# Attention stage of a graph kernel: three waits put among GpSimd's gathers of a group

## The chip, the cores and the metric

One core of a Trainium2 chip runs the whole program. The metric is device time in microseconds (us) from start to end of the program on that core; a lower number is better. Engines are named as in the profile: PE (TensorE), PEld (its weight loads), DVE (VectorE), ACT (ScalarE), POOL (GpSimd), SP (SyncE). "SPq" and "ACTq" are the DMA-issuing instructions of SP and ACT.

## The reference

A graph of 6250 nodes (128 numbers each) and 200000 edges sorted by destination goes through two layers. Only the second, attention over each node's incoming edges, is touched here:

```python
x_l = (x @ W).reshape(N, H, C)                       # H = 4 heads, C = 32
logits = leaky_relu(a_src[src_all] + a_dst[dst_all] + a_edge, 0.2)
m = segment_max(logits, dst_all)
p = exp(logits - m[dst_all])
alpha = p / segment_sum(p, dst_all)[dst_all]
out = segment_sum(alpha[:, :, None] * x_l[src_all], dst_all) + bias
```

So each edge needs the row `x_l[src]` of its source (with `a_src` beside it, 132 float32 numbers, 528 bytes), weighs it, and adds it to the sum of its destination.

## The kernel before

The edges are cut in chunks of 128 (one edge to a partition), and 15 chunks (`J`) make a group; there are 108 groups. The stage `attention` treats one group in each call of `step`; `steps` runs 8 rounds of 12 such calls in a hardware loop and the last 12 written out. Each engine has its own `step`, and they meet only in semaphores.

What one group needs, in the order of the data:

- **The source rows**, into `G`, which holds four groups. 14 or 15 chunks of a group are fetched by POOL: one indirect DMA for a chunk, 128 rows of 528 bytes, the line `pool.indirect_dma_start(...)` (L2317). One chunk of every third group is fetched by SP instead (`row_in`, L2246), as 128 DMAs of one row, with the offset of each read from a list into a register first; SP also loads the list of places of each group (`rows_of`, L2265). Two more groups of twelve have a chunk fetched in the same way by ACT, 22 rows in each step.
- **The logits** `L`: DVE adds the gathered `a_src` to what PE spread before (L2617). It waits there for all chunks of the group.
- **The running maxima** along edges of one destination: PE turns `L`, DVE scans it (L2624, L2627), PE fetches its ends (L2472, L2473), DVE reads them into `rows` (L2640) and links the chunks (L2644, L2646), PE turns back, ACT makes the exponentials.
- **The messages** `MSG`: DVE multiplies the gathered rows by the weights (L2513), as the first instruction of the next `step`.
- **The sums**: PE multiplies the messages of a chunk by its one-hot matrix (L2449), three chunks to a bank of PSUM, five banks to a group. `s_m` counts finished banks. In PE's step of group g the banks 0, 1 and 2 of group g - 1 are made in the middle and bank 3 at the very end; bank 4 follows in the next step. DVE adds each chunk to `ACC` (L2542); its first such addition for group g - 1 waits for that group's bank 0.

POOL's step for group g waits for two things: its indices (`s_i`, copied by ACT at L2392 in step g - 3) and the free place in `G` (`s_ms`, the messages of group g - 4). Then it issues all its gathers in a row. So POOL works three groups ahead of DVE. Its queue holds nothing else in this stage.

`hold` is a wait followed by an instruction that does nothing.

Of the kernel before, what the change touches and what calls it, by code (L numbers as in the profile page):

```python
# [41 lines left out]
J = 15  # L42
TRI = 3
NT = J // TRI
# [49 lines left out]
def hold(eng, semaphore, value):  # L94

    eng.wait_ge(semaphore, value)
    eng.nop(nofuse=True)
# [54 lines left out]
def build(nc, x, src, dst, edge_attr, W1l, W1r, b1, W2l, W2r, b2, gamma, beta,  # L152
          W, W_edge, att_src, att_dst, att_edge, bias, out):
    with ExitStack() as top:
# [9 lines left out]
        def sem(name, at, gathers=False):  # L164

            for n in itertools.count():
                h = at.enter_context(nc.semaphore(f"{name}_{len(stages)}" + n * "_"))
                assert h.num not in stale
                if kinds.setdefault(h.num, gathers) == gathers:
                    used.append(h.num)  # L170
                    return h
# [1932 lines left out]
        def attention(at, block):  # L2104
# [22 lines left out]
            s_m = sem("a_m", at)  # L2127
# [80 lines left out]
            END = MAX_CHUNKS - (N_GRP - 1) * J  # L2208
# [5 lines left out]
            def chunk_apart(u):  # L2214

                if u % BY_SP == BY_SP - 1:
                    return 0
                return J - 1 if u % UN in BY_ACT else None

            def places(u):  # L2220

                apart = chunk_apart(u)
                at_ = (0, J + 1, 2 * J + 3, 3 * J + 4)[u % 4] + (1 if apart is None else 0 if apart == 0 else 2)
                return G[:, at_:at_ + J, :]

            def gathered(u, last=J):

                return [j for j in range(last) if j != chunk_apart(u)]
# [9 lines left out]
            def offsets(kind, to):  # L2238

                _, v = nc.values_load_multi_w_load_instructions(  # L2240
                    to, engines=(kind,), min_val=0, max_val=(NV - 1) * ROW,
                    skip_runtime_bounds_check_because="the sources are numbers of nodes, times a row's bytes")
                return v
# [5 lines left out]
            def steps(eng, body):  # L2249

                rounds = N_GRP // UN - 1
                with eng.Fori(0, rounds) as i:
                    for u in range(UN):
                        body(i, u, UN * i + u, None)
                for u in range(UN):
                    body(rounds, u, UN * rounds + u, UN - 1 - u)
# [53 lines left out]
            @block.gpsimd  # L2310
            def _(pool):

                def step(i, u, g, left):
                    pool.wait_ge(s_i, g + 1)
                    hold(pool, s_ms, g + 1)
                    for j in gathered(u, END if left == 0 else J):
                        pool.indirect_dma_start(  # L2317
                            places(u)[:, j, :], None, x_tab, bass.IndirectOffsetOnAxis(
                                ap=idx[:, u % 4, j:j + 1], axis=0)).then_inc(s_g[u % 4], 16)
                pool.memset(BLK[:], 0).then_inc(s_bz, 1)  # L2320
                hold(pool, s_i, 2)
                pool.indirect_dma_start(places(1)[:, chunk_apart(1), :], None, x_tab, bass.IndirectOffsetOnAxis(
                    ap=idx[:, 1, chunk_apart(1):chunk_apart(1) + 1], axis=0)).then_inc(s_g[1], 16)
                steps(pool, step)
# [180 lines left out]
            def _(dve):  # L2505
# [18 lines left out]
                def blocks(g, at_, to=None):  # L2524

                    _, v = nc.values_load_multi_w_load_instructions(
                        BLK[0:1, bass.ds(g + 2, 1), at_:at_ + 8], engines=DVE_ONLY, min_val=0, max_val=NB - 1,
                        skip_runtime_bounds_check_because="a block's number counts blocks begun so far, less one")
                    if to is None:
                        blk[at_:at_ + 8] = v  # L2530
                    else:
                        to[at_:at_ + 8] = v
# [296 lines left out]
```

## Time and profile before

| | |
|---|---|
| median of 3 runs | 4956.41 us (4937.31 to 4965.21) |
| the profiled execution | 4993.1 us |
| its span, first to last instruction | 4991.3 us |
| granted TensorE clock, mean | 0.690 |
| busy: PE, DVE, ACT, POOL | 49%, 52%, 32%, 38% |
| attention stage, first to last group's messages (L2513) | 1610.3 to 4926.5 us of the span |

Two thirds of the span is the attention stage; before it lie the first layer and the projections, after it a short last stage. In the page's 40 slices DVE is at 40% and PE at 20 to 30% throughout the attention stage, POOL at 40%. A busy share of 40% says that neither engine is full; which wait ends last in a group has to be read from the timeline of one group.

### The profile page before, as it was taken

The page shows a single profiled execution, that of the slowest core. Times are in us where ns is not written, and L with a number is a line of the kernel's source. Part 1 is how long each engine was busy: PE and PEld are TensorE (multiplying, and loading weights), DVE is VectorE, ACT ScalarE, POOL GpSimd, SP SyncE. Part 2 cuts the span into 40 slices and gives each one's busy share as a digit, 9 for nine tenths or more (in the row PEclk, how much of TensorE's full clock was granted, in tenths as well). Part 3 has the DMA queues.
Part 4 walks back from the last instruction along what each step waited for, and adds up shares of the span by engine and source line. Part 5 has one row for each costly group of instructions (what it writes and reads, how often), then busy time and mean ns, then how long its engine had stood idle before and what let it go on. Part 6 is the DMA issues. An engine that isn't in the chain of part 4 may idle for free. (4 is left out here: it accounts for less than half of the span.)

```text
span 4991.3 us, 76533 instructions
## 1 busy us (share of the span) xinstructions
PE 2467.1 (49%) x19840; PEld 2062.6 (41%) x19840; DVE 2605.1 (52%) x7011; ACT 1609.9 (32%) x2523; POOL 1873.3 (38%) x1919
## 2 busy tenths in 40 slices
PE   3699999998994323323323333333333333333333
PEld 3587777877773223223223222222232322322223
DVE  2599999476754444434434444444444444444446
ACT  2487778545552212112112111111211121211121
POOL 3501113113324444444444444444444444444441
PEclk9899999999996555555555555555555555555555
DMA  3233347168883111111111111111111111111113
GB/s 114 70 160 137 150 153 177 68 226 249 252 253 123 48 52 48 47 48 52 46 48 52 46 49 49 50 47 51 50 45 52 49 46 51 49 46 52 50 47 73
DMA packets 181876, 433.71 MB, mean 87 GB/s; under 512 B 48877, under 2 KB 106074, under 8 KB 173054
## 3 DMA queue, kind: packets, MB, share of 16 engines
q1 hardware_dynamic: 68832, 273.22, 15.0%
q0 software_dynamic: 64944, 126.25, 12.2%
q10 hardware_dynamic: 47630, 28.97, 2.1%
q8 instruction: 174, 2.85, 0.2%
q14 instruction: 296, 2.42, 0.2%
HBM read 308.89 MB, written 120.97 MB: 86 GB/s over the span
## 5 line engine op out<-in xcount | busy, mean ns | idle before, releaser
L2317 POOL DMA_INDIRECT G<-x_tab,idx x1557 | 1477.3, 949 | 1859.7 <-ACT idx L2392 1393.0
L2449 PE MATMUL pu<-MSG,OH 128*128 128x140 f32 x3282 | 788.9, 415 | 118.5 <-issue 65.4
L2542 DVE TENSOR_TENSOR ACC<-pu,ACC 128x140 f32 x1641 | 486.2, 296 | 592.2 <-remote 380.6
L2449 PEld LDWEIGHTS pu<-MSG,OH 128*128 128x128 f32 x3282 | 714.6, 306 | 132.9 <-issue 73.4
L2345 ACT CAST ADG<-pt 128x180 bf16<-128x180 f32 x108 | 102.4, 948 | 1856.6 <-remote 1057.9
L2466 PE MATMUL pc<-ident,L 128*60 128x128 f32 x108 | 42.3, 391 | 867.9 <-issue 482.5
L973 ACT CAST AE<-psA 128x784 bf16<-128x784 f32 x496 | 396.6, 815 | 174.6 <-PE psA L1006 135.4
L2640 DVE COPY rows<-pc 1x120 f32<-1x120 f32 x108 | 29.2, 270 | 789.7 <-remote 717.2
L2483 PE MATMUL pc<-ident,cin 1*60 1x1 f32 x216 | 37.1, 239 | 807.6 <-DVE cbk L2646 664.8
L1107 DVE TENSOR_TENSOR OHL<-iol,LH 128x2048 bf16<-128x2048 bf16 (+1 forms) x248 | 358.1, 1444 | 71.8 <-remote 33.6
L2466 PEld LDWEIGHTS pc<-ident,L 128*60 128x60 f32 x108 | 13.7, 127 | 900.8 <-issue 900.8
L2483 PEld LDWEIGHTS pc<-ident,cin 1*60 1x60 f32 x216 | 28.0, 185 | 832.6 <-DVE cbk L2646 684.8
L1017 PE MATMUL psR<-SPL,AE 128*128 128x384 bf16 x1736 | 326.6, 329 | 1.0 <-issue 1.0
L1658 ACT CAST AR<-AE 128x896 fp32r<-128x896 bf16 x248 | 243.1, 1017 | 211.6 <-PE psR L1852 142.2
L1852 PE MATMUL psR<-SPR,AR 128*128 128x256 f32 x1922 | 285.1, 296 | 20.5 <-ACT AR L1658 16.0
L1006 PE MATMUL psA<-OHH_c,OHL 128*128 128x98 bf16 (+1 forms) x4800 | 262.7, 202 | 55.7 <-ACT AE L973 23.8
L1006 PEld LDWEIGHTS psA<-OHH_c,OHL 128*128 128x128 bf16 x4800 | 220.8, 98 | 109.1 <-issue 37.4
L1852 PEld LDWEIGHTS psR<-SPR,AR 128*128 128x128 f32 x1922 | 249.9, 193 | 36.2 <-ACT AR L1658 23.8
L2617 DVE TENSOR_TENSOR L<-G,LP 128x60 f32<-128x60 f32 x108 | 27.6, 256 | 448.5 <-issue 244.2
L2338 ACT ACTIVATE OHT<-OHT,mine 128x1920 bf16<-128x1920 bf16 x108 | 204.3, 1891 | 146.5 <-DMA OHT<-rel_tab 146.5
L1107 DVE TENSOR_TENSOR OHH_c<-ioh,LH 128x1568 bf16<-128x1568 bf16 (+1 forms) x248 | 241.1, 972 | 0.0
L2513 DVE TENSOR_TENSOR MSG<-G,pq 128x1920 f32<-128x1920 f32 (+1 forms) x109 | 231.7, 2126 | 17.3 <-issue 17.3
(435 smaller groups left out, 4783.8 us busy)
## 6 DMA issues: line engine op xcount, KB each, us to landing
a_tab<-AE SPq DMA_DIRECT2D x62, 1568.0 KB
G<-x_tab SPq DMA_DIRECT2D x4608, 0.5 KB
OHT<-rel_tab SPq DMA_DIRECT2D x108, 480.0 KB, 3.4
AE<-a_tab SPq DMA_DIRECT2D x60, 800.0 KB
AE<-a_tab SPq DMA_DIRECT2D x60, 768.0 KB
G<-x_tab ACTq DMA_DIRECT2D x2176, 0.5 KB
G<-x_tab,idx POOLq DMA_INDIRECT x1558
at_in<-in_edge_attr SPq DMA_DIRECT2D x26, 250.0 KB
```

The source lines that it names most:

```text
L973: act.copy(A[i % 2][:, :, UN_S * u:UN_S * (u + 1)].rearrange("p h (k s) -> p k h s", k=2), psA[:, n % 2, :, 0:W8].rearrange("p k (s h) -> ...
L1006: mm = pe.matmul(psA[:, n % 2, c * w // W8, to:to + w], OHL[:, m % RING, k], OHH[:, m % RING, k * step:k * step + w], start=True, stop=True)
L1017: pe.matmul(psR[:, i % 2, 0:3 * D], A[i % 2][:, h, :], SPL[:, h].rearrange("p s f -> p (s f)"), start=(h == 0), stop=False)
L1107: return dve.tensor_tensor(out.rearrange("p (s h t) -> p s h t", s=k, t=2), columns[:, 0:w].rearrange("p (h t) -> p h t", t=2)[:, None].to ...
L1658: act.copy(AR[:, n % 3, 0:len(rows_)], A[i % 2][:, rows_[0]:rows_[-1] + 1]).then_inc(s_cs, 1)
L1852: mm = pe.matmul(psR[:, i % 2, 0:2 * D], AR[:, n % 3, k], SPR[:, h - N_BF].rearrange("p s f -> p (s f)"), start=False, stop=(h == N_BLK - 1))
L2317: pool.indirect_dma_start(places(u)[:, j, :], None, x_tab, bass.IndirectOffsetOnAxis(ap=idx[:, u % 4, j:j + 1], axis=0)).then_inc(s_g[u % ...
L2338: act.activation(rows_, rows_, ACT.Square, bias=mine[:, 0:1], scale=4.0).then_inc(s_os, 1)
L2345: act.copy(ADG[:].rearrange("p j s h -> p (s h) j"), pg.rearrange("p (q j) -> p q j", j=J)).then_inc(s_ag, 1)
L2449: mm = pe.matmul(pu[:, k[0], k[1]:k[1] + MW], OH[:, u % 4, j, :], MSG[:, u % 2, j, :], start=True, stop=True)
L2513: dve.tensor_tensor(MSG[:, u % 2, 0:n, 0:XW].rearrange(x_l, h=HEADS)[:, :, :, 0:C_HEAD], places(u)[:, 0:n].rearrange(x_l, h=HEADS)[:, :, : ...
L2542: dve.tensor_tensor(a, pu[:, k[0], k[1]:k[1] + MW][:, None, :], a, ALU.add).then_inc(s_c, 1)
```

## The change

Among the gathers of one group POOL now waits three times for PE. Ahead of its eighth gather it waits until PE has made bank 0 of the message products of the group two before; ahead of the eleventh until bank 2 of that group is made; ahead of the fourteenth until bank 3 is. The values are `g * NT + 1`, `+ 3` and `+ 4` of `s_m` (`NT` is 5). The last group, which has 6 chunks, has none of these waits. Nothing else changes: the same gathers in the same order.

```diff
+                behind = {7: 1, 10: 3, 13: 4}
+
                 def step(i, u, g, left):
                     pool.wait_ge(s_i, g + 1)
                     hold(pool, s_ms, g + 1)
-                    for j in gathered(u, END if left == 0 else J):
+                    for n, j in enumerate(gathered(u, END if left == 0 else J)):
+                        if left != 0 and n in behind:
+                            hold(pool, s_m, g * NT + behind[n])
                         pool.indirect_dma_start(
                             places(u)[:, j, :], None, x_tab, bass.IndirectOffsetOnAxis(
                                 ap=idx[:, u % 4, j:j + 1], axis=0)).then_inc(s_g[u % 4], 16)
```

## Rows read from the trace of the kernel before

**Rows 1.** The page, costliest groups: busy us, mean ns, idle before and its releaser.
```profile
L2317 POOL DMA_INDIRECT G<-x_tab,idx x1557 | 1477.3, 949 | 1859.7 <-ACT idx L2392 1393.0
```

**Rows 2.** DVE's waits, 1610 to 4900: who for whom, total us, times, longest.
```profile
DVE rows L2640 <- remote: 717.2, 94, 15.7
DVE ACC L2542 <- remote: 361.3, 45, 13.3
```

**Rows 3.** Timeline of DVE over one group: start us, us, instruction, [idle before <-releaser].
```profile
3022.40 2.14 DVE L2513 TENSOR_TENSOR MSG<-G,pq 128x1920 f32<-128x1920 f32 x1
3025.37 0.25 DVE L2617 TENSOR_TENSOR L<-G,LP 128x60 f32<-128x60 f32 x1
...
3034.83 0.27 DVE L2640 COPY rows<-pc 1x120 f32<-1x120 f32 x1 [3.30 <-issue]
...
3047.58 0.30 DVE L2542 TENSOR_TENSOR ACC<-pu,ACC 128x140 f32 x1 [11.23 <-remote]
...
3052.19 2.13 DVE L2513 TENSOR_TENSOR MSG<-G,pq 128x1920 f32<-128x1920 f32 x1
```

**Rows 4.** POOL's gathers: first and last of one group's fifteen; line L2317 in sum.
```profile
3026.11 0.94 POOL L2317 DMA_INDIRECT G<-x_tab,idx  x1 [12.46 <-ACT idx L2392]
...
3043.69 0.94 POOL L2317 DMA_INDIRECT G<-x_tab,idx  x1 [0.30 <-issue]
...
L2317 POOL DMA_INDIRECT G<-x_tab,idx x1514: 942/947/1107, 1613.2 to 4884.7; - x190
```

**Rows 5.** Timeline of DVE, L2513 of the last groups, beside which POOL gathers nothing.
```profile
4897.64 2.14 DVE L2513 TENSOR_TENSOR MSG<-G,pq 128x1920 f32<-128x1920 f32 x1
...
4912.25 2.14 DVE L2513 TENSOR_TENSOR MSG<-G,pq 128x1920 f32<-128x1920 f32 x1
...
4926.46 2.14 DVE L2513 TENSOR_TENSOR MSG<-G,pq 128x1920 f32<-128x1920 f32 x1
```

**Rows 6.** SP's row DMAs, merged, and who waited for line L2246 (us, times).
```profile
2990.66 11.61 SPq L2246 DMA_DIRECT2D G<-x_tab  x32
...
3084.01 11.43 SPq L2246 DMA_DIRECT2D G<-x_tab  x32
...
4884.62 0.37 SPq L2265 DMA_DIRECT2D OHT<-rel_tab  x1
...
4897.52 0.36 SPq L2265 DMA_DIRECT2D OHT<-rel_tab  x1
4900.08 36.08 SPq L2246 DMA_DIRECT2D G<-x_tab  x96
...
  DVE L L2617: 445.4, 36
```

**Rows 7.** Row DMAs of ACT and SP around first gathers of a group, merged.
```profile
3028.51 2.99 ACTq L2246 DMA_DIRECT2D G<-x_tab  x9
...
3031.86 11.44 ACTq L2246 DMA_DIRECT2D G<-x_tab  x6
...
2995.85 6.42 SPq L2246 DMA_DIRECT2D G<-x_tab  x16
2996.45 0.94 POOL L2317 DMA_INDIRECT G<-x_tab,idx  x1 [16.45 <-ACT idx L2392]
...
3055.89 0.94 POOL L2317 DMA_INDIRECT G<-x_tab,idx  x1 [11.26 <-ACT idx L2392]
3057.16 18.02 SPq L2246 DMA_DIRECT2D G<-x_tab  x13
```

**Rows 8.** PE's message products (L2449): banks 0 to 2 and bank 3 of one step.
```profile
3029.16 4.21 PE L2449 MATMUL pu<-MSG,OH 128*128 128x140 f32 x18
...
3050.82 1.75 PE L2449 MATMUL pu<-MSG,OH 128*128 128x140 f32 x6
```

**Rows 9.** Timeline of DVE in a group with SP's chunk: messages, then logits.
```profile
2987.43 2.13 DVE L2513 TENSOR_TENSOR MSG<-G,pq 128x1920 f32<-128x1920 f32 x1
...
3003.48 0.26 DVE L2617 TENSOR_TENSOR L<-G,LP 128x60 f32<-128x60 f32 x1 [13.00 <-issue]
```

## The prediction

> **What bounds the kernel now.** I read the page first, then DVE's waits, then the timeline of one group on every engine. The page gives POOL 1557 gathers of 949 ns with most of its idle time spent waiting for ACT's indices [rows 1]: POOL isn't full, and it works three groups ahead. DVE's long waits sit at two places, the copy of `rows` (L2640) and the first addition of a bank (L2542), both released by a signal of PE [rows 2]. In the group that begins at 3022.40 the logits come at +2.97, `rows` at +12.4 and the next addition only at +25.2, after 11.23 us of nothing; the group ends at +29.8 [rows 3]. PE made what that addition waits for in the products that began at 3029.16, that is at +6.8 [rows 8]. So PE had long been done, and the releaser named isn't the cause. What does fit is POOL: its fifteen gathers run from 3026.11 to 3043.69 + 0.94 = 3044.63, one every 17.58 / 14 = 1.256 us [rows 4], and DVE goes on 2.95 us after the last has ended [rows 3]. Where POOL gathers nothing a group takes 14.6 and 14.2 us [rows 5], less than half of 29.8. I read this as a state, "starved", in which the other engines get hardly anything done while gathers are in flight.
>
> The starved state shows best in the row DMAs. ACT issues 9 rows in 2.99 us (0.33 each), then 6 in 11.44 (1.9 each); SP in another group 13 in 18.02 (1.39 each) [rows 7]. Without gathers SP does 96 rows in 36.08 us with its register loads, 0.376 each [rows 6]. So a starved SP runs at about 0.33 / 1.39 = 24% of its speed and loses 0.76 us in each starved microsecond.
>
> **SP is the bound behind it.** SP fetches 128 rows for every third group. From the 32 rows at 2990.66 to the like ones at 3084.01 are 93.35 us for three groups [rows 6]; DVE waited for line L2246 in all 36 such groups, 445.4 us in sum, 12.4 each [rows 6], as in the 13.00 us ahead of the logits at 3003.48 [rows 9]. Undisturbed, SP needs 36.08 for 96 rows and 4897.52 - 4884.62 = 12.90 for 32 more [rows 6], 49.0 in all. The other 44.4 us, 14.8 per group, is lost to starvation. A change that shortens DVE's group but not the starved time gives nothing: DVE then waits longer for SP in each third group.
>
> **The change part by part.** Nothing is removed and the 1557 gathers keep their length; the three waits cost POOL well under 1 us each, and behind them in POOL's queue stand only the gathers themselves. The gathers move. Bank 3 of group g - 2 is made at the end of PE's step g - 1: the six products at 3050.82 end at 3052.57, 0.4 us into the next group [rows 3, 8]. With 0.8 us of response, estimated from gaps like those in rows 4, POOL starts at +1.2: the last one or two gathers of group g (needed at once), then seven of g + 1. That run of 8 or 9 ends near 1.2 + 9 x 1.256 = +12.5. The eighth of g + 1 needs bank 0, a third of the 18 products, so ready at 3029.16 + 1.40 = 3030.56, 5.2 us after the logits [rows 3, 8]; the eleventh needs bank 2, 2.8 us later [rows 8], less than three gathers take (3.8 us): I expect gathers 8 to 13 as one run of 6. So the lead of three groups is gone, and a group has two runs (9 and 6) where bank 0 comes after +12.5, and one run of 15 where it comes before.
>
> *Logits.* Gathers 14 and 15 are issued at +1.2 and +2.5 and end at +3.4. Landing isn't in the rows; the 2.95 us between the last end and DVE's restart [rows 3, 4] bounds it above, 0 below. I take 1.3, so the logits come at +4.7, 1.7 us later than now. On DVE's chain this is covered by starvation that then starts 2.5 us earlier too (+1.2 for the first gather against 3026.11 - 3022.40 = +3.7 [rows 3, 4]): a run of 15 would end at +19.7 and free the engines at +22.7 instead of +25.2. DVE's group would be about 27.5 instead of 29.8, and SP's 31.1 (93.35 / 3) bounds it.
>
> *Starved time.* A run of n gathers starves for 1.25 n - 0.3 + 2.95 less a grace at its start. The grace is 5.4 us by ACT (3026.11 to 3031.5), 5.8 by SP (2996.45 to 3002.3), but 1.3 by SP in the next group but one (3055.89 to 3057.16) [rows 4, 7]. Cutting a run in two adds one tail of 2.65 and one grace: the starved time changes by 2.65 - 5.8 = -3.2 to 2.65 - 1.3 = +1.4 us, SP's time by 0.76 of it, -2.4 to +1.0. I take the middle, a grace of 3.5: -0.65 us per cut.
>
> *How many cuts.* The 36 groups with SP's chunk surely have one: their logits come at +16 [rows 9], bank 0 some 5 us later, and POOL stands from +12.5 on. In the other 69 gathering groups bank 0 is due at 4.7 + 5.2 = +9.9 if PE isn't starved, which gives no cut, and later if it is. I take half, 35. Together 71 x 0.65 = 46 us.
>
> *Ends of the stage.* The first gathers no longer run three groups ahead before the first messages, and some 13 gathers come back beside the last groups; the number of starved microseconds is the same, so zero, within about 20 us.
>
> A rule of the Trainium skill speaks against the change: the page "DMA: Bandwidth & Descriptors", section "Rules for kernel authors", says to issue a DMA early, compute, and wait late, since the fixed cost of its set-up is hidden so. By its roughly 2 us of fixed cost the logits of every group would come about as late as my 1.7 us, and nothing would hide it. No row of this case has shown the landing of a lone gather.
>
> **The rivals.**
> 1. *The grace is long in every run.* Every group is cut once at the 5.4 us that ACT's rows show: (5.4 - 2.65) x 0.76 = 2.1 us, x 105 = 220 us: 4993 - 220 = 4773, or 4736 at the median. For: two of three rows. Against: SP's budget, where 14.8 lost / 0.76 = 19.5 us starved per group leaves for 14.7 gathers only 18.4 + 2.65 - 19.5 = 1.5 us of grace.
> 2. *No cut, SP as before.* PE's products come ahead of +12.5 in ordinary groups, the runs stay whole, and the cuts of the others pay for their tails: 4956, within 25 us.
> 3. *Slower: each pause starts a new starved stretch at once.* Place: SP's rows, right after a pause of POOL. With the 1.3 us of grace the price is 1.0 us per cut, x 71 to 105 = 71 to 105 us, 5027 to 5061. It decides from a grace below 2.65 us.
> 4. *Slower: late logits.* The early-issue rule as a mechanism of this kernel: the logits wait for gathers 14 and 15, and the engines aren't freed earlier, so two of three groups grow by 1.7 us: 105 x 2/3 x 1.7 = 119 us, 5075. It needs a chain of DVE that is longer than SP's 93.35 us in three groups; at present it has some 4 us of slack in three.
>
> That the change doesn't do what it says is excluded: now POOL gathers for three groups ahead, and it can't with these waits.
>
> **How the numbers follow.** The sum is against the profiled execution: 4993.1 - 46 = 4947. The median of the runs shown lies 36.7 us lower, so 4910. Chances: forecast 0.32, rival 1 0.15, rival 2 0.25, rival 3 0.20, rival 4 0.08. The range goes from rival 1's 4740 to 5050, inside rival 3's prices. About 0.5% (25 us) is what a measurement of this kernel can tell from no change. Faster 0.32 + 0.15 = 0.47, same 0.25, slower 0.28. As both signs hold much of it: the forecast's own range is 4840 to 4930.
>
> **What would show it.** In the profile after: POOL's L2317 released by PE, not by ACT, with a first gather near +1.2; runs of 9 and 6 with a pause in the groups with SP's chunk; logits near +4.7 in ordinary groups; the three-group distance of SP's 32-row bursts at 93 less one to two us. The prediction is wrong if SP's distance falls far below 90 us (then the grace is the whole story), if the logits' wait for L2246 vanishes, or if DVE still waits until +25 with gathers already over.

## The result, and the profile after

| | before | after |
|---|---|---|
| median (range), us | 4960.81 (4937.31 to 4968.49) | 4535.57 (4533.08 to 4548.93) |
| profiled execution's span, us | 4991.3 | 4547.1 |
| first to last start of the messages (L2513, now L2517), us | 3338.0 | 2919.9 |
| granted TensorE clock | 0.690 | 0.713 |

The changed kernel takes 0.9155 of the time before, interval 0.913 to 0.9179: 425 us less, against a forecast of 4910 us and a range of 4740 to 5050. Of the profiled executions' difference, 444 us, 418 lie in the attention stage. All lines below the change now stand four higher in number (L2317 is L2321, L2617 is L2621). The stage is read from the messages' line (ns least, median, most; first and last start), before and after:

```profile
L2513 DVE TENSOR_TENSOR MSG<-G,pq x109: 945/2135/2155, 1610.3 to 4948.3; 128x1920 f32<-128x1920 f32 x108, 128x768 f32<-128x768 f32 x1
```

```profile
L2517 DVE TENSOR_TENSOR MSG<-G,pq x109: 946/2134/2156, 1584.2 to 4504.1; 128x1920 f32<-128x1920 f32 x108, 128x768 f32<-128x768 f32 x1
```

The page of the kernel after, costliest groups (busy us, mean ns of one, idle before and what ended most of it), answers to [rows 1]:

```profile
L2321 POOL DMA_INDIRECT G<-x_tab,idx x1557 | 1470.8, 945 | 1450.2 <-PE pu L2453 695.2
L2546 DVE TENSOR_TENSOR ACC<-pu,ACC 128x140 f32 x1641 | 484.1, 295 | 151.3 <-issue 76.0
L2621 DVE TENSOR_TENSOR L<-G,LP 128x60 f32<-128x60 f32 x108 | 28.0, 259 | 780.2 <-DMA G<-x_tab 624.2
```

The gathers are as many and as long. They are now released by PE's products, and the long waits of the additions are gone. DVE's and POOL's waits (who for whom, us in sum, times, longest) answer to [rows 2]:

```profile
DVE L L2621 <- DMA G<-x_tab: 624.2, 36, 20.6
DVE rows L2644 <- remote: 148.1, 69, 3.3
DVE L L2621 <- DMA G<-x_tab,idx: 126.0, 62, 4.0
...
POOL G L2321 <- PE pu L2453: 695.2, 79, 19.0
...
POOL G L2321 <- remote: 344.4, 135, 3.7
```

The wait ahead of `rows` fell from 717.2 us to 148.1, its longest from 15.7 to 3.3. What grew is the wait for SP's row DMAs: 624.2 us in 36 groups, 17.3 each, against 445.4 [rows 6].

POOL's timeline over the group that begins at 2722.72 (start us, us, instruction, idle before and its releaser) answers to [rows 4]:

```profile
2726.38 0.94 POOL L2321 DMA_INDIRECT G<-x_tab,idx  x1 [2.45 <-remote]
...
2736.37 0.94 POOL L2321 DMA_INDIRECT G<-x_tab,idx  x1 [0.30 <-issue]
2740.38 0.94 POOL L2321 DMA_INDIRECT G<-x_tab,idx  x1 [3.07 <-PE pu L2453]
...
2746.61 0.94 POOL L2321 DMA_INDIRECT G<-x_tab,idx  x1 [0.30 <-issue]
2750.05 0.94 POOL L2321 DMA_INDIRECT G<-x_tab,idx  x1 [2.49 <-remote]
```

A run of nine, a pause of 3.07 us, a run of six that reaches over the group's end, a pause of 2.49. The 79 + 135 waits for PE and its like ("remote") among POOL's are about two pauses in each of the 105 groups; the trace has 105 runs of six and 107 of eight or nine. In each third group, where DVE waits for SP's rows, the pause behind the longer run is far longer, up to the 19.0 us above. Before, a group had one run of fourteen or fifteen and one pause of 11.26 to 16.45 us [rows 4, 7]. DVE's timeline over the same group and the two that follow answers to [rows 3] and [rows 9]:

```profile
2722.72 2.13 DVE L2517 TENSOR_TENSOR MSG<-G,pq 128x1920 f32<-128x1920 f32 x1
...
2731.20 0.26 DVE L2621 TENSOR_TENSOR L<-G,LP 128x60 f32<-128x60 f32 x1 [2.98 <-DMA G<-x_tab,idx]
...
2739.53 0.27 DVE L2644 COPY rows<-pc 1x120 f32<-1x120 f32 x1 [1.29 <-remote]
...
2745.46 2.13 DVE L2517 TENSOR_TENSOR MSG<-G,pq 128x1920 f32<-128x1920 f32 x1
...
2752.61 0.26 DVE L2621 TENSOR_TENSOR L<-G,LP 128x60 f32<-128x60 f32 x1 [0.70 <-DMA G<-x_tab,idx]
...
2767.62 2.13 DVE L2517 TENSOR_TENSOR MSG<-G,pq 128x1920 f32<-128x1920 f32 x1
2791.82 0.26 DVE L2621 TENSOR_TENSOR L<-G,LP 128x60 f32<-128x60 f32 x1 [17.91 <-DMA G<-x_tab]
```

The two ordinary groups take 22.74 and 22.16 us, against 29.8 before. The third, with SP's chunk, has its logits only at +24.2 (before +16.0 [rows 9]) and gives a part back. Taken over 99 groups of the stage, the two ordinary kinds take 20.8 and 22.8 us in the mean (before 30.0 and 29.8) and the kind with SP's chunk 38.6 (before 34.6). PE's products in the first of these groups answer to [rows 8]:

```profile
2735.09 2.57 PE L2453 MATMUL pu<-MSG,OH 128*128 128x140 f32 x12
2738.29 0.98 PE L2453 MATMUL pu<-MSG,OH 128*128 128x140 f32 x6 [0.63 <-DVE ACC L2546]
```

SP's row DMAs, merged (the first two rows are from narrow windows, inside and behind the run of six), answer to [rows 6]:

```profile
2741.79 6.47 SPq L2246 DMA_DIRECT2D G<-x_tab  x6
...
2748.97 3.13 SPq L2246 DMA_DIRECT2D G<-x_tab  x11
...
2778.48 12.18 SPq L2246 DMA_DIRECT2D G<-x_tab  x32
...
2861.06 12.10 SPq L2246 DMA_DIRECT2D G<-x_tab  x32
```

The three-group distance is 2861.06 - 2778.48 = 82.58 us, against 93.35.

### The profile page after: what moved, and what is told of

Same layout as the page of the kernel before. It is cut to its first block and busy times, and to the rows that moved or that the text cites. A ratio compares the mean times of both kernels' runs of the same rounds, so it can differ in the third digit from the quotient of the medians.

```text
span 4547.1 us, 77142 instructions
## 1 busy us (share of the span) xinstructions
PE 2418.7 (53%) x19840; PEld 2020.2 (44%) x19840; DVE 2620.4 (58%) x7011; ACT 1599.4 (35%) x2523; POOL 1867.0 (41%) x1919
## 5 line engine op out<-in xcount | busy, mean ns | idle before, releaser
L2321 POOL DMA_INDIRECT G<-x_tab,idx x1557 | 1470.8, 945 | 1450.2 <-PE pu L2453 695.2
L2453 PE MATMUL pu<-MSG,OH 128*128 128x140 f32 x3282 | 765.3, 407 | 42.1 <-DVE ACC L2546 18.0
L2453 PEld LDWEIGHTS pu<-MSG,OH 128*128 128x128 f32 x3282 | 695.2, 298 | 55.7 <-DVE ACC L2546 24.8
L2621 DVE TENSOR_TENSOR L<-G,LP 128x60 f32<-128x60 f32 x108 | 28.0, 259 | 780.2 <-DMA G<-x_tab 624.2
L1006 PE MATMUL psA<-OHH_c,OHL 128*128 128x98 bf16 (+1 forms) x4800 | 261.3, 202 | 52.1 <-DVE OHH_c L1107 24.2
L1852 PEld LDWEIGHTS psR<-SPR,AR 128*128 128x128 f32 x1922 | 249.0, 193 | 33.0 <-ACT AR L1658 22.6
L2517 DVE TENSOR_TENSOR MSG<-G,pq 128x1920 f32<-128x1920 f32 (+1 forms) x109 | 231.6, 2125 | 19.0 <-issue 19.0
L2511 DVE TENSOR_TENSOR OH<-pq,REL 128x1920 f32<-128x1920 f32 x108 | 232.0, 2148 | 2.5 <-issue 2.5
L1844 PE MATMUL psR<-SPB,AE 128*128 128x384 bf16 x1116 | 220.7, 335 | 15.4 <-DMA AE<-a_tab 12.0
L920 POOL DMA_INDIRECT srows<-src_pad,EKI x34 | 60.6, 1782 | 358.4 <-DVE KB L1089 188.5
```

The costliest lines, as they stand in the source:

```text
L1006: mm = pe.matmul(psA[:, n % 2, c * w // W8, to:to + w], OHL[:, m % RING, k], OHH[:, m % RING, k * step:k * step + w], start=True, stop=True)
L1844: mm = pe.matmul(psR[:, i % 2, 0:3 * D], A[i % 2][:, h, :], SPB[:, h].rearrange("p s f -> p (s f)"), start=(h == 0), stop=False)
L1852: mm = pe.matmul(psR[:, i % 2, 0:2 * D], AR[:, n % 3, k], SPR[:, h - N_BF].rearrange("p s f -> p (s f)"), start=False, stop=(h == N_BLK - 1))
L2321: pool.indirect_dma_start(places(u)[:, j, :], None, x_tab, bass.IndirectOffsetOnAxis(ap=idx[:, u % 4, j:j + 1], axis=0)).then_inc(s_g[u % ...
L2453: mm = pe.matmul(pu[:, k[0], k[1]:k[1] + MW], OH[:, u % 4, j, :], MSG[:, u % 2, j, :], start=True, stop=True)
L2511: dve.tensor_tensor(OH[:, u % 4], rowq[:, None, :].to_broadcast([P, J, P]), REL[:, bass.ds(g * J, J)][:, :, None].to_broadcast([P, J, P]), ...
```

## The experiments

The theory after the result, called Cut: the starved state (the other engines get hardly anything done while gathers are in flight) holds as I described it, and each cut of a run of fifteen gathers is worth far more than the 0.65 us that I took. Rivals: Place (what helps is that the gathers start at the end of PE's step and no longer run three groups ahead), and SP against DVE (is it SP's rows, slowed by the gathers, that set the pace, or DVE's own chain?). In diffs, `behind` is the table that the change adds: {number of the gather, counted from zero: bank that it waits for}.

### Four kernels where nothing was starved

Their ratios need one sentence first: the kernel before, run beside them, took 3461.35 us (16 runs, 3453.08 to 3479.5), not 4961. Nothing in the kernel differs. The chip does, as far as it is on record: these four ran on chip 0, the eight further down where the kernel before takes about 4960 us on chips 12 and 11.

Only the wait ahead of the fourteenth gather:

```diff
-                behind = {7: 1, 10: 3, 13: 4}
+                behind = {13: 4}
```

> Only the wait ahead of the fourteenth gather. Gathers 14 and 15 of a group, 1 to 13 of the next: one run of 15, begun 1.2 us into the group. Theory 'cut' (the gain is that the run of 15 is cut in two, and SP's row DMAs are the bound): as before the change, 4930 to 4970 us, three-group distance of SP's bursts 93 us. Rival 'place' (the gain is that gathers begin right after bank 3 instead of after ACT's indices): most of the gain is here, about 4600 us.

Measured: 3485.53 us, ratio 1.0059 (1.003 to 1.0089).

Without the eleventh's wait, `behind = {7: 1, 13: 4}`:

> The waits ahead of the eighth and fourteenth, not the one ahead of the eleventh. Both theories: bank 2 is ready when the tenth gather has been issued, so runs of 9 and 6 as in the changed kernel and its time, 4535 +- 15 us. If the eleventh's wait makes a cut of its own it is slower by 50 us or more.

Measured: 3481.03 us, 1.0055 (1.0035 to 1.0075).

Without the eighth's wait, `behind = {10: 3, 13: 4}`:

> The waits ahead of the eleventh and fourteenth, not the eighth: runs of 12 (2 + 10) and 3. Theory 'cut', starved time falls by a fixed amount for each cut: as the changed kernel, 4535 us. If instead the starved time grows faster than the run's length (a backlog), a run of 12 is worse than 9 and 6: 4650 to 4800 us. Rival 'place': 4535 to 4600 us.

Measured: 3473.4 us, 1.0042 (1.0011 to 1.0074).

The kernel before with one wait ahead of the tenth gather and the lead of three groups kept. PE raises a semaphore of its own behind banks 0 to 2, and it starts three ahead:

```diff
+            s_q = sem("a_q", at)
...
+                        if left != 0 and n == 9:
+                            hold(pool, s_q, g + 1)
...
+                pe.sem_inc(s_q, 3)
...
                     sums(g - 1, u - 1, (0, 1, 2))
+                    pe.sem_inc(s_q, 1)
```

> The kernel before with one wait, ahead of the tenth gather, for a signal that PE raises behind the products of banks 0 to 2 of its current step; POOL still works three groups ahead. Runs of 9 and 6, nothing late for the logits. Theory 'cut': 4450 to 4540 us, at least the whole gain, as the logits no longer wait for gathers 14 and 15. Rival 'place': no gain, 4900 to 4960 us.

Measured: 3461.89 us, 1.0003 (0.9991 to 1.0014). Its trace shows what is different there: first the messages' line (L2518), then POOL's waits, then SP's row DMAs merged.

```profile
L2518 DVE TENSOR_TENSOR MSG<-G,pq x109: 946/2134/2155, 1474.1 to 3409.3; 128x1920 f32<-128x1920 f32 x108, 128x768 f32<-128x768 f32 x1
```

```profile
POOL G L2320 <- issue: 474.9, 1556, 0.3
```

```profile
2452.18 10.24 SPq L2247 DMA_DIRECT2D G<-x_tab  x32
2462.66 0.36 SPq L2266 DMA_DIRECT2D OHT<-rel_tab  x1
2465.33 10.61 SPq L2247 DMA_DIRECT2D G<-x_tab  x32
```

POOL never stands: 1556 gathers follow their forerunners after 0.3 us, one each 1.25 us, and 1557 x 1.25 = 1946 us is the whole stage (1474.1 to 3409.3, 1935 us). SP issues 32 rows in 10.24 us in the midst of these gathers, 0.32 each, where a starved SP needed 1.39 [rows 7]. So in these four runs the starved state doesn't exist, POOL is the bound, and the changed kernel's waits can only cost: 0.4 to 0.6%, some 12 to 24 us. The wait of the fourth kernel is never waited for. None of the expectations, all made for a starved execution, is tested here.

### The change again, one wait, and half of SP's rows, where it starves

For the next four the kernel before took 4955.93 us (7 runs, 4942.99 to 4968.43). First the change itself:

> The changed kernel once more, beside the kernel before. The last four kernels ran where the kernel before took 3461 us and its traces showed no starved stretch (32 of SP's row DMAs in 10 us with gathers in flight, gathers at a pitch of 1.25 us without a break). Theory A (the gain is relief of starvation and nothing else): where the kernel before takes about 4960 us the ratio is 0.915 as measured first; where it takes about 3461 us, the ratio is 1.004 to 1.006, like the kernels with one or two of the waits. Rival B (the change helps by the order of the gathers, whatever the starvation): under 0.98 in both places.

Measured: 4540.95 us, 0.9169 (0.9142 to 0.9195), 415 us less. That is theory A where the state is present. For where it is absent, the change itself wasn't run; the kernel without the eleventh's wait, which turns out to be its equal (below), took 1.0055 there.

Only the fourteenth's wait, `behind = {13: 4}`:

> Only the wait ahead of the fourteenth gather. Where the kernel before takes about 4960 us: theory Cut (each cut of the run of fifteen in two gives SP some 3.8 us, and the place of the pause doesn't matter): this one has no pause inside the run of fifteen, only a run that starts later, so it gains little, 0.98 to 1.01. Rival Place (what helps is that the gathers no longer start three groups ahead and run right beside the products): 0.93 or less with this wait alone. Where the kernel before takes about 3461 us: 1.006 again, and it tells nothing.

Measured: 4846.65 us, 0.9772 (0.9735 to 0.9809), 109 us less. Neither had it right: a run of fifteen is never cut, yet the kernel gains beyond Cut's 0.98. DVE over one ordinary group, and the first and last gather of its run:

```profile
2968.47 2.13 DVE L2517 TENSOR_TENSOR MSG<-G,pq 128x1920 f32<-128x1920 f32 x1
2973.57 0.26 DVE L2621 TENSOR_TENSOR L<-G,LP 128x60 f32<-128x60 f32 x1 [2.05 <-DMA G<-x_tab,idx]
2991.05 0.27 DVE L2644 COPY rows<-pc 1x120 f32<-1x120 f32 x1 [11.04 <-remote]
...
2997.19 2.14 DVE L2517 TENSOR_TENSOR MSG<-G,pq 128x1920 f32<-128x1920 f32 x1
```

```profile
2969.62 0.95 POOL L2321 DMA_INDIRECT G<-x_tab,idx  x1 [10.01 <-PE pu L2453]
...
2987.14 0.94 POOL L2321 DMA_INDIRECT G<-x_tab,idx  x1 [0.30 <-issue]
```

The run goes from +1.2 to +19.6, and DVE is freed at +22.6, 2.97 us behind its end. The group takes 28.7 us instead of 29.8. That is Place, at a quarter of the gain.

The wait ahead of the tenth with the lead kept, diff as above:

> The kernel before with one wait ahead of the tenth gather, on PE having made banks 0 to 2 of the group in hand; the lead of three groups stays. Where the kernel before takes about 4960 us: theory Cut: two runs, 9 and 6, per group, 3.8 us per cut of SP's time, so 0.92 to 0.95. Rival Place: lead unchanged, so no gain, 0.99 to 1.01. Where the kernel before takes about 3461 us: 1.000 again, and it tells nothing.

Measured: 4834.24 us, 0.9753 (0.9721 to 0.9784), 122 us less, half of what Cut expected. POOL's waits say why:

```profile
POOL G L2320 <- ACT idx L2395: 1131.5, 104, 19.6
...
POOL G L2320 <- PEq L2485: 130.1, 33, 5.3
```

My signal (L2485) held POOL 33 times only (the timeline has 34 runs of nine and 35 of five, the other runs are whole). In about two of three groups PE had made banks 0 to 2 before the run starved it, and the run stayed whole. 121.7 / 33 = 3.7 us for each cut (3.5 with 35), the lead being kept. So the price per cut was right and the count was wrong. The cut runs all have 14 gathers, and stand at each third group, as SP's chunk does: the price is that of a cut in those groups, and says nothing of the others.

Half of SP's row DMAs, each writing its row to two partitions:

```diff
-                        for m in range(PER_LOAD):
-                            row_in(sp, (BY_SP * k + BY_SP - 1) % UN, low + m, v[m], s_sr[k % (UN // BY_SP)])
+                        for m in range(0, PER_LOAD, 2):
+                            w, p = (BY_SP * k + BY_SP - 1) % UN, low + m
+                            sp.dma_start(places(w)[p:p + 2, chunk_apart(w), :].bitcast(U8),
+                                         x_bytes[:, bass.ds(v[m], ROW)].to_broadcast([2, ROW])
+                                         ).then_inc(s_sr[k % (UN // BY_SP)], 16)
...
-                        dve.wait_ge(s_sr[u // BY_SP], 16 * P * (i + 1))
+                        dve.wait_ge(s_sr[u // BY_SP], 8 * P * (i + 1))
```

> The kernel before with half of SP's row DMAs: each fetches one row and writes it to two partitions, so every second row of SP's chunk is not the one that the reference uses (that part of the computation is left out). Theory SP (SP's row DMAs are the bound behind the starved stretches): where the kernel before takes about 4960 us, a three-group period of 93 us falls to DVE's own chain, about 3 x 29.7 = 89 less the 13 us for which DVE waited on SP in one of three: ratio 0.90 to 0.96. Rival PE/DVE (the bound is DVE's own starved chain and SP's waits are only its echo): 0.99 to 1.00. Where the kernel before takes about 3461 us, SP isn't the bound by its trace: 0.99 to 1.00.

Measured: 4757.03 us, 0.9601 (0.9573 to 0.9628), at the upper edge of theory SP's range. SP's rows are a bound, by about 199 us.

### Which wait does it, and SP's rows taken away

The kernel before took 4967.17 us here (9 runs, 4921.54 to 4975.63). Only the eighth's wait, `behind = {7: 1}`:

> Only the wait ahead of the eighth gather, on bank 0. Known so far where the kernel before takes about 4956 us: all three waits 0.917, only the wait ahead of the fourteenth 0.977 (runs of 15, never cut), one wait ahead of the tenth with the lead kept 0.975 (only 34 of 105 runs cut, that is 3.6 us per cut). Theory Cut (3 to 3.6 us of SP's time per cut of a run, on top of 1 us per group for a start bound to PE): the eighth waits until bank 0, near +10, and the first seven of the next group wait for ACT's indices near +3.7 of that group: if they form two runs, 8 and 7, in all groups, 0.92 to 0.94; if the two join to one run of 15, 0.97 to 0.98 as with the fourteenth alone. Rival (the fourteenth's wait matters since it ties the gathers to the end of PE's step): 0.99 to 1.00. Where the kernel before takes about 3461 us: 1.000 to 1.006.

Measured: 5007.2 us, 1.0104 (1.0063 to 1.0146), 40 us more, outside all that was expected. DVE's waits, its timeline at the start of a group, and the gathers of the run beside it:

```profile
DVE LP L2608 <- remote: 1152.6, 106, 13.5
```

```profile
2888.88 2.13 DVE L2517 TENSOR_TENSOR MSG<-G,pq 128x1920 f32<-128x1920 f32 x1
2902.83 0.34 DVE L2608 TENSOR_REDUCE LP<-px 128x60 f32<-128x180 f32 x1 [11.81 <-remote]
```

```profile
2881.44 0.94 POOL L2321 DMA_INDIRECT G<-x_tab,idx  x1 [20.06 <-PE pu L2453]
...
2898.94 0.95 POOL L2321 DMA_INDIRECT G<-x_tab,idx  x1 [0.31 <-issue]
2911.60 0.95 POOL L2321 DMA_INDIRECT G<-x_tab,idx  x1 [11.71 <-PE pu L2453]
```

The two parts join to one run of fifteen, which starts 7.4 us ahead of the group's end and so lies on the head of the next group's chain: DVE waits at `LP`, its first step behind the messages, until 2902.83, 2.94 us behind the run's end, and the whole chain is still to come. What a wait is worth doesn't lie in the wait, but in whether it makes a pause in a run, and where the run lies.

Without the eleventh's wait, `behind = {7: 1, 13: 4}`:

> The waits ahead of the eighth and fourteenth gather, without the one ahead of the eleventh. The traces of the changed kernel show no pause at the eleventh: gathers 8 to 13 are one run of six. Where the kernel before takes about 4956 us: theory Cut: the same as all three, 0.915 to 0.92. Rival (all three waits count, each a third of the gain left): 0.93 to 0.95. Where the kernel before takes about 3461 us: 1.0055 again.

Measured: 4540.93 us, 0.9154 (0.9104 to 0.9205): the change itself. The eleventh's wait does nothing, and the eighth's, which by itself costs 40 us, is worth 306 us (4846.65 - 4540.95) once the fourteenth's keeps the parts from joining.

GpSimd gathers the chunk of every third group as well, and SP fetches no rows, on the changed kernel and on the kernel before:

```diff
-                if u % BY_SP == BY_SP - 1:
-                    return 0
                 return J - 1 if u % UN in BY_ACT else None
...
-                        for m in range(PER_LOAD):
-                            row_in(sp, (BY_SP * k + BY_SP - 1) % UN, low + m, v[m], s_sr[k % (UN // BY_SP)])
...
-                    if u % BY_SP == BY_SP - 1:
-                        dve.wait_ge(s_sr[u // BY_SP], 16 * P * (i + 1))
```

> The changed kernel, but GpSimd also gathers the chunk of every third group that SP fetches row by row (36 gathers more, 4608 row DMAs of SP fewer; the output is the reference's). In the changed kernel ordinary groups take 19 to 24 us and the groups with SP's chunk 36 to 43, with 624 us of waits for SP's rows. Theory SP (SP's row DMAs, slowed by the gathers in flight, are the bound): every group takes about 21.5 us and one gather more in a third of them, 105 x 21.5 + 45 = 2300 us in place of 105 x 27.3 = 2870: about 3970 us, ratio 0.78 to 0.84 against before. Rival DVE (the chain of the engines is the bound and SP's waits are its echo): 0.90 to 0.92. Where the kernel before takes about 3461 us: GpSimd is the bound there, 36 x 1.25 = 45 us more, ratio 1.015 to 1.02.

Measured: 4072.78 us, 0.8197 (0.8153 to 0.8241).

> The kernel before, but GpSimd also gathers the chunk that SP fetches (the output is the reference's). With half of SP's row DMAs it took 0.960. Theory SP for the kernel before: ordinary groups take 29.7 us and all of them would now, 105 x (31.1 - 29.7) = 147 us, and 45 more for the gathers: ratio 0.95 to 0.98; nothing more, since DVE's own starved group is the next bound. Together with the kernel above it tells whether the waits and SP's load act on one another: if the gain of the waits alone (0.917) grows without SP's chunk, the waits help DVE's chain too; if it shrinks, they helped by SP. Where the kernel before takes about 3461 us: 1.01 to 1.02.

Measured: 4745.55 us, 0.9564 (0.952 to 0.9608). The messages' line in either kernel, first the one with the waits:

```profile
L2513 DVE TENSOR_TENSOR MSG<-G,pq x109: 942/2135/2156, 1586.4 to 4048.2; 128x1920 f32<-128x1920 f32 x108, 128x768 f32<-128x768 f32 x1
```

```profile
L2509 DVE TENSOR_TENSOR MSG<-G,pq x109: 944/2135/2156, 1601.2 to 4712.3; 128x1920 f32<-128x1920 f32 x108, 128x768 f32<-128x768 f32 x1
```

| us per group (stage / 108) | with SP's rows | without |
|---|---|---|
| before | 30.9 | 28.8 |
| with the three waits | 27.0 | 22.8 |

The waits save 3.9 us per group with SP's rows and 6.0 without. So they don't need SP's rows to gain: they shorten DVE's starved chain, and SP's rows hide a third of it. Rival DVE (0.90 to 0.92 for the first kernel) is out. SP was the bound before by 2.1 us per group and is so by 4.2 after. The kernel with the waits and without SP's rows is the fastest of all, and beats the change by 10%, where the state exists.

Where the 6 us come from can be read from the changed kernel's DVE and POOL above. From `rows` (2739.53) to the next messages (2745.46) DVE's chain takes 5.9 us, with the run of six beside it from 2740.38 on; in the kernel with the fourteenth's wait alone the same stretch takes 6.1 us (2991.05 to 2997.19) with no gather beside it. Over the stage the medians are 6.2 and 5.8 us. So the end of the chain isn't held by the first four or five gathers of a run, and the cut puts five gathers beside it where POOL stood idle before. That this is the whole of the 6 us is an inference; no run moves the run of six alone.

### Six runs for lead and length that met no starved state

The last two sets were to tell cut from lead, and number from length of the runs. The kernel before took 3462.25 us beside the first four (on chip 2) and 3464.16 beside the last two (on chip 10), so both questions stayed open, and what these runs give is the price of each form where POOL is the bound. The first of them repeats `behind = {10: 3, 13: 4}`:

> The waits ahead of the eleventh and the fourteenth gather only: runs of 12 and 3 in place of 9 and 6, if the signal of bank 2 reaches GpSimd only after the run, as bank 0's does in the changed kernel. Where the kernel before takes about 4960 us: theory Gaps (an ordinary group is the gathers' own 1.25 us each plus one gap of some 3.5 us behind each run, whatever its length): 13.75 + 3.9 + 2.5 + 3.4 = 23.5 us against 23.0 with 9 and 6, so the same within 1%: 0.915 to 0.925. Rival Length (a run is starved only from its fourth microsecond on, so a run of 3 isn't starved at all and the run of 12 is so for long): SP then gets about as much in the sum; but if the backlog of a long run is what costs, 0.93 to 0.95. If bank 2's signal comes in time, there is no cut and it takes 0.977, as with the wait ahead of the fourteenth alone. Where the kernel before takes about 3461 us: 1.004 again.

Measured: 3480.26 us (six runs, 3477.15 to 3557.06), 1.006 (1.0036 to 1.0083).

`behind = {4: 0, 13: 4}`:

> Waits ahead of the fifth gather (on the bank that PE makes first in its step) and of the fourteenth: runs of 6 and 9 in place of 9 and 6. Where the kernel before takes about 4960 us: theory Gaps and theory Cut: the same as the change, 0.91 to 0.925, since runs and gaps are as many and as long. Rival (what helps is where in the step the pause lies, beside the products of banks 0 to 2): 0.94 to 0.98. Where the kernel before takes about 3461 us: 1.00 to 1.01.

Measured: 3501.99 us, 1.0119 (1.0093 to 1.0145), 40 us more. Waits in these places cost a POOL that is the bound about twice as much.

The kernel with the lead kept, its signal moved behind the products of `cin` and `cbk`:

```diff
...
                    sums(g - 1, u - 1, (0, 1, 2))
-                    pe.sem_inc(s_q, 1)
...
                               start=True, stop=True).then_inc(s_col, 1)
+                    pe.sem_inc(s_q, 1)
```

> The kernel before with one wait ahead of the tenth gather, as in the kernel with the lead kept, but on a signal that PE gives later in its step, after the products with cin and cbk, which come only once DVE has been freed of the run. So GpSimd keeps its lead of three groups and every run should be cut (9 and 6), not only 34 of 105. Where the kernel before takes about 4960 us: theory Cut (the cut is worth 3 to 3.6 us and the lead nothing): 0.92 to 0.94. Rival Lead (the change gains since the gathers start right at the end of PE's step): 0.975 as with 34 cuts or higher. Where the kernel before takes about 3461 us: 0.998 to 1.003.

Measured: 3461.54 us, 1.0001 (0.9989 to 1.0014).

The changed kernel with every chunk gathered by GpSimd, ACT's too:

```diff
             def chunk_apart(u):
-                if u % BY_SP == BY_SP - 1:
-                    return 0
-                return J - 1 if u % UN in BY_ACT else None
+                return None
...
-                        for m in range(PER_LOAD):
-                            row_in(sp, (BY_SP * k + BY_SP - 1) % UN, low + m, v[m], s_sr[k % (UN // BY_SP)])
...
-                    for m in some:
-                        if m < len(v):
-                            row_in(act, to_act[u // HALF_A], u % HALF_A * PART_A + m, v[m], s_ar[u // HALF_A])
+                    pass
...
```

> The changed kernel with all chunks gathered by GpSimd: neither SP nor ACT fetches rows (the output is the reference's). With SP's rows gone it took 0.820, 4073 us, and ACT's rows are left (128 in every sixth group). Theory (a group is now 15 gathers and two gaps, 18.75 + 2 x 2.2 = 23 us, and ACT's 128 rows cost DVE only in the groups that wait for them): 18 gathers more, 23 us, and up to 18 x 4 us less: 0.80 to 0.82. Rival (ACT's slowed rows hold up its other work in all groups, as SP's did): under 0.79. Where the kernel before takes about 3461 us: 1.02 to 1.03.

Measured: 3543.43 us, 1.0226 (1.0201 to 1.025), 81 us more: 54 more gathers x 1.25 = 68, and the waits. It says what a POOL-bound execution charges when GpSimd gathers everything; on the starved side this kernel stays untried.

The two open ones once more:

> As before for this kernel: the lead of three groups kept, one wait ahead of the tenth gather on a signal that comes late in PE's step, so that every run is cut. Where the kernel before takes about 4960 us: theory Cut 0.92 to 0.94; rival Lead 0.975 or higher. Where it takes about 3461 us: 1.000, which the last set has shown already.

Measured: 3462.3 us, 0.9995 (0.9982 to 1.0008).

> As before for this kernel: runs of 12 and 3. Where the kernel before takes about 4960 us: theory Gaps 0.915 to 0.925; rival Length 0.93 to 0.95; no cut 0.977. Where it takes about 3461 us: 1.006, which two sets have shown already.

Measured: 3475.87 us, 1.0033 (1.0021 to 1.0046).

## Why the prediction was wrong

**The starved state: right.** DVE comes back 2.94 to 2.97 us behind the end of a run of fifteen in three kernels, and nothing of the gain appears where the state doesn't (1.0055 against 0.9154 for the same file). That the state is there on some chips and not on others, I had no row for.

**POOL's new course: the runs right, their start and the number of cuts wrong.** PE releases POOL, and the runs are of nine or eight and six. But the run of nine starts at 2726.38 and 2750.05, +3.7 and +4.6 of their groups, and not at +1.2: bank 3 was made in time, and its signal came late, since the run of six that had just ended still held the engines. (In the kernel with the fourteenth's wait alone, where POOL had long been idle by then, the start is at +1.2 as predicted.) And "71 cuts" failed. I expected bank 0 at +9.9 in ordinary groups and half of them uncut. The products began at 2735.09, +12.4, and POOL was released only at 2740.38, 4.0 us behind the end of bank 0's share of them (a half of 2.57 us): this signal, too, came once the run had let go. So all 105 groups were cut.

**The saving per cut: the term that was mis-sized.** I took 0.65 us; the waits that cut measure 306 / 105 = 2.9 us each, and 3.7 with the lead kept. The part that fell is the tail: I gave each of the two runs the 2.95 us of a run of fifteen. After the run of nine DVE goes on at 2739.53, 2.2 us behind its end (2737.31), and after the run of six SP's fast rows begin at 2748.97, 1.4 us behind 2747.55. With 2.2 + 1.4 in place of 2 x 2.95, a cut changes the starved time not by 2.65 less the grace but by 0.3 less the grace, with my grace of 3.5 by -3.2 us, and by 0.76 of it SP's time: -2.4 us. That alone makes 105 x 2.4 = 252 us. The trace agrees when SP's slow steps are added up (steps of line L2246 that take 0.55 us or more, over 99 groups): 15.8 us per group before, 15.7 with the fourteenth's wait alone, 13.0 with all three. Thus 2.7 us less for a cut, and SP's time in row DMAs falls by 2.9 (26.1, 26.1, 23.2 us per group), against the 2.9 measured. The grace of 3.5 was a lucky middle between unlike values: a run of six slows SP from 1.4 us on (median of 105), a run of nine from 4.8, a whole run of the kernel before from about 3. The first two, less the last that was there already, are 3.2.

SP isn't slowed by the rows alone. Between two bursts it also waits for signals of the starved engines. Before, merged rows of SP in one triple of groups:

```profile
2803.27 12.78 SPq L2246 DMA_DIRECT2D G<-x_tab  x32
2820.31 0.01 SPq L2265 DMA_DIRECT2D OHT<-rel_tab  x1
2825.96 12.35 SPq L2246 DMA_DIRECT2D G<-x_tab  x32
```

From the end of the first burst to the start of the next are 9.9 us, where the unstarved execution above shows 2.9 (2462.42 to 2465.33). I had put all of the 44.4 us lost per three groups down to slow rows. Over the stage SP spends 5.4 us per group outside its row DMAs before, 4.2 with the fourteenth's wait alone and 4.2 with all three.

**"A change that shortens DVE's group but not the starved time gives nothing": the step that failed.** I had the shorter group nearly right, 27.5 us (by its own terms 27.3) with DVE freed at +22.7 for an uncut run that starts at +1.2; measured in the kernel with the fourteenth's wait, 28.7 and +22.6. But I set it at zero, since SP's 31.1 us stood above it. It was worth 109 us. SP's time isn't a fixed sum beside DVE's. Its slow steps indeed stayed as they were (15.8 and 15.7 us per group); what shrank is its time outside the row DMAs, by 1.2 us per group (5.4 to 4.2), which is what a group became shorter, and which I had taken as fixed. Adding up, 109 + 306 = 415, the measured gain; I had 0 + 46: the first term put at nothing for a wrong reason, the second too small by its tail, and by its count of cuts (71 for 105).

**The rivals.** Rival 1, every group cut with a long grace, had the number of cuts and the order of size of each (2.1 us), and still fell short by half: the tail, and the 109 us of the earlier start, which it doesn't have. Rival 2, no cut, is out. Rival 3, slower by a new starved stretch behind each pause, has its place in the kernel with the eighth's wait alone, where the run moved onto the head of the chain. Rival 4: the late logits did come, later than I feared (+8.5 and +7.1 where they had been at +2.97, since the run starts so late), and the groups with them are 7 us shorter all the same. The rule of the Trainium skill (page "DMA: Bandwidth & Descriptors", section "Rules for kernel authors"), issue early and wait late, agrees with the runs in which nothing was starved: the waits of the change, all or some, cost 0.3 to 0.6% there, and the kernels that kept the lead nothing (1.0003, 1.0001). Where the gathers starve the others it didn't decide.

**The landing of a gather.** I had bounded it by 0 and 2.95 us and taken 1.3 behind the recorded end. The logits at 2731.20 start 2.6 us behind the end of the gather of 2727.63 (2728.57), on which they wait; in about half of such groups of this kernel it is 1.6 to 1.8 us, as it is in most of the kernel with the fourteenth's wait alone. The Trainium skill (page "Perfetto Trace Analysis", section "DMA Instruction — SWDGE (GPSIMD)") says that the end recorded for such an instruction is that of writing its descriptors, and not of moving the data; the trace agrees.

**What would show it.** "Released by PE" and "9 and 6" came as said. SP's distance, 82.58 us, lies far below 90, which I had named beforehand as the sign that the prediction is wrong and the grace the whole story; the cut, with its tail and grace, is three quarters of it, 306 of 415 us. The first gather near +1.2 and the logits near +4.7 did not come.

**Still open.** Whether cutting every run with the lead kept gives 0.92 to 0.94 (only its third, 33 cuts at 3.7 us, is measured), whether 12 and 3 or 6 and 9 do as well as 9 and 6, so whether the number of cuts counts or their place, and why the same kernel starves on one chip and not on another.

## What to carry to other kernels

When an engine's products are long done and its consumer still waits, look at what else is in flight: here the wait's end lay 2.95 us behind the last of a row of gathers, whoever was named as releaser. Then ask of a wait not what it holds up but what it makes of the run behind it, cut in two or moved onto the head of the chain: the same wait was worth 306 us in company and cost 40 alone. And a bound that is itself slowed by the state that a change relieves, or waits for the engines in it, is no floor: compute it anew with the change, before calling a gain ahead of it zero.

## What the runs showed of the hardware

- Runs of GpSimd's gathers in flight slow the other engines on some chips and not on others. The kernel before took 4956 to 4967 us in three sets of runs (two of them on chips 12 and 11, the chip of the first isn't on record) and 3461 to 3464 in three (chips 0, 2 and 10), their single runs within about 1%, with the same gathers of 0.94 us at a pitch of 1.25 us. The kernel before was never in between, and a set held one or the other throughout. No chip was used twice, so the chip and the hour aren't told apart, and the cause isn't in the traces. The data don't move more slowly: over the stage a packet of GpSimd's queue took 0.14 us in the mean in the kernel before and 0.155 where nothing was starved (kernel with the lead kept), one of the largest hardware queue 0.11 in both.
- The tail by which SP stays slowed behind a run grows with the run. Medians: 1.1 us behind five gathers and 1.9 behind nine (lead kept), 1.3 behind six, 1.6 behind eight and 1.85 behind nine (the change), 2.6 to 2.9 behind fourteen or fifteen. DVE comes back a little later, in the groups shown 2.2 behind nine and 2.95 behind fifteen.
- Not all engines are held from the same moment. Behind the start of a run of six SP is slow from 1.4 us on, while DVE, PE and ACT finish the chain up to the messages, which start at 5.3 us (medians of the change), nearly at the pace that they have without gathers (6.2 us from `rows` to the messages against 5.8).
- A slowed SP takes up to 0.70 us for each of its instructions, the register move as well as the DMA, against medians of 0.03 and 0.23. The line in the changed kernel from 2736 to 2775 (ns: least, median, most):

```profile
L2246 SPq DMA_DIRECT2D G<-x_tab x59: 4/228/700, 2736.5 to 2775.0; - x59
L2246 SPq MOVE G<-x_tab x58: 4/29/707, 2737.9 to 2774.9; - x58
```

Two of them make the 1.39 us of a starved row [rows 7]. It isn't the DMA that is slow but the engine's steps from one instruction to the next, which fits that products already made, and their signals, come late too.
